# One more convolution tap on TensorE, gate rows folded into weights kept in DRAM, three transposed-input buffers with x loaded a chunk ahead, and softplus at steps 25 and 29

## The reference

```python
mod = (_silu(c) @ wmod).reshape(B, 6, 1, -1)          # sa, ca, ga, sb, cb, gb
ga, gb = (2 * (g >= 0) - 1) * maximum(abs(g), 0.25)   # for both gates
h = _layernorm(x) * (1 + ca) + sa
x = x + ga * mamba(h)
h = _layernorm(x) * (1 + cb) + sb
x = x + gb * (einsum('btd,rde->bte', h, factors) / sqrt(8) + bias)
```

```python
h, gate = split(h @ in_proj.T)
h = silu(causal depthwise conv of 4 taps over time (h) + conv_b)
dt, Bp, Cp = split(h @ x_proj.T)                      # 128, 16, 16
dt = softplus(dt @ dt_proj.T + dt_proj_b)
s  = s * exp(dt * A) + (dt * h) * Bp                  # scan over time, per channel and state
y  = (sum over states of s * Cp + h * D) * silu(gate)
return y @ out_proj.T
```

## Time and profile before

| | |
|---|---|
| median of 3 runs | 2041.11 us (2040.35 to 2041.86) |
| profiled execution | 2039.69 us, its span 2038.0 us |
| VectorE (DVE) busy | 1886.0 us, 93% |
| GpSimd (POOL) busy | 1859.4 us, 91% |
| TensorE (PE) busy | 1753.2 us, 86% |
| ScalarE (ACT) busy | 1501.1 us, 74% |
| granted TensorE clock, mean | 0.956 |
| DMA queue of SyncE | 174.85 MB, 25.2% of 16 engines' span |

### The profile page before, as it was taken

The page is one execution under the profiler, slowest core; times in us unless marked ns, Lnnn a source line. Parts: engine busy times, 40 slices in busy tenths (PEclk is TensorE's granted clock), DMA queues, the critical chain, the costliest instruction groups (busy, mean ns, idle before and its releaser), DMA issues.

```text
span 2038.0 us, 28861 instructions
## 1 busy us (share of the span) xinstructions
PE 1753.2 (86%) x8872; PEld 1288.6 (63%) x8872; DVE 1886.0 (93%) x2343; ACT 1501.1 (74%) x4602; POOL 1859.4 (91%) x924
## 2 busy tenths in 40 slices
PE   7887888989888898988979789798988979799798
PEld 4666656667665666656666575666657666576664
DVE  2898999999999999999999899999999999999995
ACT  3777687776877777787777777777787777877663
POOL 0889999999999999999998999999999999999993
PEclk9898999989999998999999989999999999999798
DMA  4647304041230404123142230404113041310300
GB/s 169 238 84 193 96 31 147 22 155 42 94 99 27 156 22 142 56 79 104 38 145 73 102 109 29 150 27 140 57 72 110 32 145 37 122 60 28 119 27 31
DMA packets 71599, 184.04 MB, mean 90 GB/s; under 512 B 6674, under 2 KB 8338, under 8 KB 63252
## 3 DMA queue, kind: packets, MB, share of 16 engines
q1 hardware_dynamic: 67748, 174.85, 25.2%
q0 software_dynamic: 3696, 7.34, 2.2%
HBM read 172.20 MB, written 9.96 MB: 89 GB/s over the span
## 4 chain that ended last, share of the span: by engine, by line
DVE 32%; ACT 18%; POOL 17%; PE 16%; issue 15%; DMA 1%; DVEq 0%; POOLq 0%; SPq 0%; ACTq 0%
DVE decay L1362 11%; POOL ub L541 9%; DVE state_p L1362 9%; ACT decay L666 6%; POOL state_p L569 5%; DVE sc_d L1377 5%; PE bank_c L1092 4%; PE y_bank L949 3%; ACT dt L772 2%; DVE bank_a L1417 2%; ACT L666 2%; ACT L772 2%; PE bank_a L1039 1%; PE bank_c L1119 1%; ACT xa L681 1%
## 5 line engine op out<-in xcount | busy, mean ns | idle before, releaser
L541 POOL TENSOR_TENSOR ub<-u,b_all 128x2048 f32<-128x2048 f32 x255 | 1164.5, 4567 | 48.2 <-DMA b_all<-bc_scratch 48.2
L666 ACT ACTIVATE decay<-dt,decay_rate 128x256 f32<-128x256 f32 (+1 forms) x2048 | 888.9, 466 | 81.1 <-DVE state_p L1362 78.7
L1362 DVE TENSOR_TENSOR_SCAN decay<-decay,carry,ub 128x512 f32<-128x512 f32 x584 | 725.9, 1274 | 16.9 <-ACT decay L666 15.5
L1362 DVE TENSOR_TENSOR_SCAN state_p<-decay,carry,ub 128x512 f32<-128x512 f32 x440 | 559.5, 1273 | 45.1 <-ACT decay L666 45.1
L569 POOL TENSOR_TENSOR state_p<-state_p,c_all 128x1024 f32<-128x1024 f32 (+2 forms) x256 | 529.2, 2067 | 60.3 <-ACT carry L650 49.6
L949 PE MATMUL y_bank<-ident,sc_d 128*128 128x128 f32 x2336 | 361.4, 289 | 141.9 <-DVE sc_d L1377 141.8
L949 PEld LDWEIGHTS y_bank<-ident,sc_d 128*128 128x128 f32 x2336 | 279.9, 148 | 218.5 <-DVE sc_d L1377 212.4
L1377 DVE TENSOR_TENSOR sc_d<-decay,c_all 128x512 f32<-128x512 f32 x584 | 388.8, 670 | 0.0
L650 ACT ACTIVATE carry<-decay 128x2 f32<-128x2 f32 x584 | 95.7, 164 | 340.0 <-DVE sc_d L1377 340.0
L949 PEld LDWEIGHTS y_bank<-ident,state_p 128*128 128x128 f32 x1760 | 212.4, 146 | 96.1 <-POOL state_p L569 50.6
L949 PE MATMUL y_bank<-ident,state_p 128*128 128x128 f32 x1760 | 248.7, 283 | 26.4 <-POOL state_p L569 23.5
(11 more groups left out here) (138 smaller groups left out, 1858.9 us busy)
## 6 DMA issues: line engine op xcount, KB each, us to landing
win_h<-win_m SPq DMA_DIRECT2D x128, 256.0 KB, 2.6
win_z<-win_m SPq DMA_DIRECT2D x128, 256.0 KB, 2.7
b_all<-bc_scratch SPq DMA_DIRECT2D x31, 1024.0 KB, 6.1
c_all<-bc_scratch SPq DMA_DIRECT2D x31, 1024.0 KB, 7.1
xa<-x SPq DMA_DIRECT2D x16, 512.0 KB, 4.0
xc<-x SPq DMA_DIRECT2D x16, 512.0 KB, 3.7
out<-xc SPq DMA_DIRECT2D x15, 512.0 KB, 6.8
ffn<-factors POOLq DMA_DIRECT2D x7, 1024.0 KB, 9.1
```

What stands on the lines that cost most here:

```text
L541: pool.tensor_tensor(ub[:, slot, :, :, :], u[:, (PAIRS * c + q) % U_PAIRS, :, :].unsqueeze(1).to_broadcast([P, QUAD, 2, ROWS]), b_all[:, n ...
L666: last = act.activation(bk[:, j * ROWS + j:(j + 1) * ROWS], dt[:, pair % DT_PAIRS, j, j:], ACT.Exp, scale=decay_rate[:, e, n:n + 1])
L1362: dve.tensor_tensor_scan(dst, bk[:, :], ub[:, quad % UB_RING, i, :, :].rearrange("p j r -> p (j r)"), carried_in[:, n, 2 * q:2 * q + 1], A ...
```

## The change

- **Taps.** VectorE keeps one tap (`DVE_TAPS = 1`, two instructions a pair), and TensorE has two (`PE_TAPS`, four matmul calls a pair). The diagonals are made on GpSimd before the first chunk (`make_diagonals`), two instructions, and no longer on ScalarE.
- **Split of the C multiplies.** The tuples give GpSimd 27 and 26 units in plain chunks where it had 29 and 28, 19 and 23 in the first two chunks where it had 21 and 26, and 414 in all where it had 440. `EARLY` moves from units 46 and 54 to units 50 and 58.
- **Gates.** ga and gb have no memory of their own: they lie in `y_rows` and `xc` for a while in the first round. In the first two rounds GpSimd multiplies the weights by the second batch entry's gates into spare buffers (`keep_wo`, four, and `keep_ffn`, two), SyncE stores these in DRAM, and GpSimd then scales the weights in place for the first entry (`scale_wo`, `scale_ffn`). In rounds 8 and 9 the finished weights are loaded; nothing is scaled there. The bias is scaled for both entries at once.
- **Inputs.** `hT` has three buffers, and the second layer norm's transposed rows go there and not into `xa`. So x is loaded a chunk earlier: statistics at steps 25, 26 and 28 and `z_before` at step 30 of the round two before its chunk, `turn_x` at step 31, `modulate_before` at step 1, `project_h` at steps 1 to 4 and 7 to 10 (from 5 to 8 and 10 to 13).
- **The pair work of the next chunk** moves three steps up, except in round 0: `copy_h` and `taps` to steps 5, 7, 10, 12, `add_tap` to 6, 8, 11, 13, tanh and `silu_before` to 7, 9, 12, 14. `project_out` stands at steps 9 to 15 (was 8 to 16). `project_dt` starts at step 16, `copy_dt` and `copy_bc` are at 22 and 23 (were 20 and 21), `expand_dt` at 22, 23, 26, 27 (were 19, 20, 23, 24).
- **Softplus** groups are at steps 25 and 29. `stats_before` (two instructions) stands between the two scans of step 25, and `add_ffn(c - 1, 1)` between those of step 29.

```diff
-PE_TAP = 2
-TAP_STEPS = 2 * PE_TAP
+DVE_TAPS = 1
+PE_TAPS = range(DVE_TAPS, TAPS - 1)
+H_RING = 3
+H_LATE = 3
+M_AT = (2, 1)
+IN_AT = ((2, 3, 4, 5, 7, 8, 9, 10), (1, 2, 3, 4, 7, 8, 9, 10))
-EVEN_POOL = (2, 2, 2, 2, 2, 2, 3, 2, 2, 2, 2, 1, 2, 1, 1, 1)
-ODD_POOL = (2, 2, 2, 2, 2, 2, 2, 2, 2, 2, 2, 1, 2, 1, 1, 1)
+EVEN_POOL = (2, 2, 2, 2, 2, 2, 2, 2, 2, 2, 2, 1, 1, 1, 1, 1)
+ODD_POOL = (2, 2, 2, 2, 1, 2, 2, 2, 2, 2, 2, 1, 1, 1, 1, 1)
-EARLY = (46, 54)
+EARLY = (50, 58)
...
+            def keep_wo(i):
+                if i == 0:
+                    pool.wait_ge(wo_loaded, 16)
+                    pool.wait_ge(rows_made, BATCH)
+                wait(pool, wo_stored, 16 * i)
+                pool.tensor_tensor(spare[2], wo[:, 2 * i:2 * i + 2, :], ga[:, 1:2, :].to_broadcast([P, 2, DIM]),
+                                   ALU.mult).then_inc(wo_kept, 1)
...
+            def make_diagonals():
+                pool.wait_ge(prep, 3)
+                pool.wait_ge(consts_made, 1)
+                for i, k in enumerate(PE_TAPS):
+                    pool.tensor_tensor(tap_diag[:, i, :, :], ident[:, :].unsqueeze(1).to_broadcast([P, KE, P]),
+                                       conv[:, :, k:k + 1].to_broadcast([P, KE, P]), ALU.mult).then_inc(diag_made, 1)
...
-                    if c == 0 and g in (7, 9, 11, 13):
-                        scale_wo(0, g // 2 - 3)
-                    if c == PER and g in (11, 12, 13, 14):
-                        scale_wo(1, g - 11)
-                    if c % PER == 1 and g in (4, 5):
-                        scale_ffn(c // PER, g - 4)
+                    if c == 0 and g in (6, 7, 9, 10):
+                        keep_wo({6: 0, 7: 1, 9: 2, 10: 3}[g])
+                    if c == 0 and g in (7, 8, 9, 11):
+                        scale_wo({7: 0, 8: 1, 9: 2, 11: 3}[g])
+                    if c == 1 and g in (2, 4):
+                        keep_ffn(g // 2 - 1)
+                    if c == 1 and g in (3, 5):
+                        scale_ffn(g // 2 - 1)
...
                 for j in range(2):
-                    last = pe.matmul(h_lane(c, q)[:, j * ROWS:(j + 1) * ROWS], tap_diag[:, 2 * q + j, :],
-                                     pre[q % 2][:, j, PE_TAP:PE_TAP + ROWS], start=False, stop=True, skip_group_check=True)
+                    for i, k in enumerate(PE_TAPS):
+                        last = pe.matmul(h_lane(c, q)[:, j * ROWS:(j + 1) * ROWS], tap_diag[:, i, 2 * q + j, :],
+                                         pre[q % 2][:, j, k:k + ROWS], start=False, stop=(k == TAPS - 2),
+                                         skip_group_check=True)
...
+                    if c + 2 < CHUNKS and s == 25:
+                        stats_before(c + 2)
+                    if lc is not None and s == 29:
+                        add_ffn(c - 1, 1)
```

More of the change, by code:

```diff
@@ L429, in one_round @@
                     load_z(c, m)
[L430 to L437, removed]
+                if c >= 2:
+                    load_xc(c - 1)
+                if c + 2 < CHUNKS:
+                    load_xa(c + 2)
                 if c == PER + 1:
@@ new lines, in scale_wo, with keep_ffn @@
+            def scale_wo(i):
+                pool.wait_ge(wo_kept, i + 1)
+                part = wo[:, 2 * i:2 * i + 2, :]
+                pool.tensor_tensor(part, part, ga[:, 0:1, :].to_broadcast([P, 2, DIM]), ALU.mult).then_inc(wo_scaled, 1)
+            def keep_ffn(i):
+                if i == 0:
+                    pool.wait_ge(fac_added, 16 * (RANK - 1))
+                    pool.wait_ge(rows_made, 2 * BATCH)
+                    pool.wait_ge(c_full[1], 2)
+                wait(pool, ffn_stored, 16 * i)
+                pool.tensor_tensor(spare[0], ffn[:, 2 * i:2 * i + 2, :], gb[:, 1:2, :].to_broadcast([P, 2, DIM]),
+                                   ALU.mult).then_inc(ffn_kept, 1)
@@ L600, in one_round @@
                     quad = QUADS * c + g
-                    if la is not None and g == 0:
-                        norm_before(c + 1)
+                    if c == 0 and g == 0:
+                        norm_before(1)
+                    if c + 2 < CHUNKS and g == 13:
+                        norm_before(c + 2)
                     if lc is not None and g == 9:
@@ L773, in soft_dt, with seam_decays @@
                 last.then_inc(dt_made, 1)
-            def seam_decays(c, par):
-                act.wait_ge(dt_made, PAIRS * c + PAIRS)
+            def seam_decays(c, par, half):
+                act.wait_ge(dt_made, PAIRS * c + 2 * half + 2)
                 wait(act, ub_made, QUADS * (c - 1) - 1)
-                for q in range(PAIRS):
+                for q in (2 * half, 2 * half + 1):
                     e, slot = 2 * q + 1, (PAIRS * c + q) % DT_PAIRS
@@ L1240, in one_round @@
                 for s in range(STEPS):
-                    if la is not None and s in (9, 11, 14, 16):
-                        add_tap(c + 1, {9: 0, 11: 1, 14: 2, 16: 3}[s])
+                    a = s - H_LATE if c == 0 else s
+                    if la is not None and a in (6, 8, 11, 13):
+                        add_tap(c + 1, {6: 0, 8: 1, 11: 2, 13: 3}[a])
                     turn_states(STEPS * c + s)
@@ L1410, in taps @@
                 dve.wait_ge(pre_made, PAIRS * c + q + 1)
-                for k in range(PE_TAP):
+                for k in range(DVE_TAPS):
                     for j in range(2):
```

322 lines of the change are left out of this document (174 added, 148 removed).

## The result

The changed kernel takes 2103.3 us (median of 4 runs, 2096.63 to 2109.9) against 2041.11: a ratio of 1.0305, interval 1.0266 to 1.0344. It is 3% slower, where I had forecast 2002 us and a chance of 0.88 for faster. Its profiled execution took 2098.99 us, with a span of 2097.3.

A forecast was written before the change was run, and what follows sets the result against it. VectorE's queue was taken to set the pace, GpSimd hardly behind. Twelve plain rounds -29.3, round 9 -10.4, rounds 0 and 1 +1 sum to -38.7 us: 2002 forecast, own range 1990 to 2012, wider range 1974 to 2028.

The forecast's parts named there:

- costed at nothing: Items given no time: GpSimd's diagonals, lead-in taps, the later B and C round trip, reloads in rounds 8 and 9, tail.
- account of rounds 0 and 1: Gate folding on GpSimd in the first two rounds: 260.5 us together, +1, bounds -4 and +15.
- waits for TensorE in steps 5 to 9: Sign that the forecast is wrong, listed beside no wait at step 12 and others; no size given.
- The rival in which TensorE's order decides: Plain rounds: longer taps before each tanh and the shared steps 1 to 4 give 123.6 us a round, 2070; chance 0.09.
- The waits of a plain round: VectorE's waits in a plain round: 3.7 us against 4.3 before, on 114.7 of work, giving 118.4.
- The third pair: Steps 12 and 13: TensorE's late, longer tap makes VectorE wait 1.4 us for tanh, `pre` or decay; bounds 0 and 3.0.
- The norm in step 19: VectorE's wait for the norm: no term in the plain round's sum, and no such wait expected.
- Step 29: VectorE's wait for ScalarE's decay behind the softplus group, with `add_ffn` in between: 0.6 us, bounds 0 and 1.8.
- the rival in which the waits only move: Plain rounds: the taps' 1.9 us a round return as other VectorE waits, 120.9 a round, 2034 us; chance 0.06.
- The rival with 1977: GpSimd's pace: third pair's lateness hidden, plain rounds at 116.4 us, 1977 in all; chance 0.25.
- the +15 of that rival: Rounds 0 and 1: folding costs its full price, +15 us in place of +1, 2016 in all; chance 0.10.
- Round 9: Loses its `ffn` scaling and the lag from round 8, becoming a plain round: 118.4 us against 128.8, -10.4.

The follow-up runs named there:

- experiment one: Changed kernel with SyncE loading `win_h` tiles 3 to 5 ahead of the gate tiles and both x loads: 2038.71 us, ratio 0.9982 to the kernel before.
- Experiments two to four: Changed kernel, `win_h` tiles 3 to 5 behind the gate tiles: ahead of both x loads, 2040.86 us; behind `xc` only, span 2057.7; behind `xa` only, span 2053.0.
- Experiment six: Kernel of experiment one with the output projection's first four jobs at steps 9, 11, 12, 12, not 9 to 12: 2022.38 us, ratio 0.9911 to the kernel before.
- experiment seven: Kernel of experiment six with one scan product more a round given to GpSimd: span 2019.1 us against 2019.2.
- experiment ten: Changed kernel with all three repairs: late weight tiles first, output projection jobs spread, gate's last tanh ahead of the copy in step 5: 2012.43 us, ratio 0.9863.

## Why the prediction was wrong

**The step that failed** is in the "costed at nothing" and in the account of rounds 0 and 1: I followed SyncE's queue there and in the B and C trip, and nowhere else. The loads of `win_h` in a plain round thus went into the sum at nothing, without a reason. The change moves two things towards each other. The projection of the fourth tile goes from step 8 to step 4, and the load of `xa` goes ahead of the late `win_h` tiles in the queue, where only that of `xc` had been. No sentence of mine asked when the fourth tile lands in a plain round. In its place the runs showed a tile that is 3.6 us late on average in rounds 2 to 14, which costs 58.1 us by experiment one, some 22 of them by the lower clock behind the wait (the estimate above). Experiments two to four show that the bytes in front do it. One of my signs of being wrong was waits for TensorE in steps 5 to 9, and it came, in step 6. The rival in which TensorE's order decides named the moved projection, but for its matmuls and not for its weights. It came nearest to the time, 2070, for another reason, which is luck, and I gave it 0.09.

**The waits of a plain round** are the second step that failed. With the loads put right (experiment one) they are 6.1 us on average over the twelve, and not 3.7. Before the change they were 4.3. Three terms were off:
- The third pair, forecast 1.4, measured 2.3. The mechanism is the one forecast. Seven us of TensorE's work lie between the first of the two projections and the tap (605.22 to 612.54, 7.3 us, the sum that I made), but the first one starts 1.7 us after `silu_before` (603.51) and not 0.7, since the transposes of the states, which end at 605.22, stand in front. That makes the tap a us later than forecast, which is about the missing 0.9. Experiment six removes 1.6 of the 2.3.
- The norm in step 19, forecast 0, measured 1.0. I had only counted the norm of the input side, whose wait did go, and GpSimd's slack of 2.7 us a round. But slack on average doesn't help at one place. GpSimd is behind at step 19. With one product more for it the wait grew from 0.7 to 1.1 us (experiment seven). It may also hang on a carry that it waited for earlier, which I have not shown.
- Step 29, forecast 0.6, measured between 0.46 and 1.56, 0.9 on average.

The waits in step 22 (forecast 0.8, measured 0.89), step 30 (0.3 and 0.2) and step 5 (0.4 and 0.40) came as forecast, step 25 nearly so (0.2 and 0.4). So did the work: a plain round of 120.8 us less its waits of 6.1 is 114.7, as forecast.

With its loads in time, the change is then the rival in which the waits only move: forecast 2034, measured 2038.7, which is still outside my range. VectorE's work falls by the 1.9 us a round that were forecast, its waits rise by 1.9, and the plain rounds are as long as before. The rival with 1977 needed the lateness at the third pair to be hidden, and it was not: 2.3 us of waiting. That GpSimd's work paces the rounds is refuted by experiment seven for the kernel of experiment six.

**Rounds 0 and 1**, forecast 260.5, measured 268.2. Of the +8.8 on before, 3.0 is the late tile in round 1 (127.5 in experiment one). Round 1 is 2.9 us shorter than before without it, and round 0 is 8.7 us longer. I had put GpSimd in round 0 at 126.9 of work and 5 of idle time. It has 126.1 and 11.6, and over 10 of these are waits for a carry, as before the change; I had taken them for waits for the mods and softplus. The idle time that I meant to fill can't be filled by work that stands behind the wait in the same queue. The folding is dear, but at +5.8 it is not the +15 of that rival.

**Round 9** was right in its mechanism, hidden under the late tile: it has become a plain round, 121.8 us beside an average of 120.8 in experiment one and 118.4 beside 118.6 in experiment ten. That its 118.4 is the forecast figure needed the three repairs. **The lead-in** grew by 1.9 where I had 0 for it.

The forecast of 118.4 us for a plain round and -10.4 for round 9 is what the kernel with all three repairs does, and that is partly luck. Its waits sum to 3.9 us a round for the forecast 3.7, but from other terms: 0.7 for 1.4 in step 12, 0.7 for 0 in step 19, 1.1 for 0.6 in step 29 and none for 0.4 in step 5. Of three new latenesses (the tile, the third pair, the norm) I had found one, and priced it too low.

## What to carry to other kernels

When an operation is moved earlier, write down for each of its operands when it now has to be there, and read the queue that brings it: what stands in front, and how many bytes. Here 1 MB in front of a 256 KB tile cost 58 us, more than the 39 that the whole change was forecast to bring. Part of that price was indirect: in 10 of 13 rounds TensorE ran at a lower clock behind its wait. A large transfer that nobody waits for belongs behind a small one that somebody does, and that is an edit of three lines.

When work goes off the engine that seems to be the bound, and the rounds stay as long as they were, list the bound engine's waits by step. In the three places mended here (the late tile, the third pair, the gate's tanh) the cure was the order of another queue, and cost nothing.

## What was not expected of the hardware

The scaling of the bias has two operands in SBUF and 512 elements in a row, on two partitions. VectorE in the changed kernel, round 0:

```profile
144.91 10.14 DVE L1542 SCALAR_TENSOR_TENSOR bias_row<-bias_row,dt 2x512 f32<-2x512 f32 x1
154.98 1.27 DVE L1424 TENSOR_TENSOR_SCAN decay<-decay,carry,ub 128x512 f32<-128x512 f32 x1
```

The kernel before has the same multiply on one partition, and it took 0.67 and 0.89 us. The long one is no accident of one execution: it took 9.94 us in experiment one and 10.07 in experiment eleven.

GpSimd at that time:

```profile
143.72 2.83 POOL L612 TENSOR_TENSOR wo<-wo,y_rows 128x1024 f32<-128x1024 f32 x1
146.04 4.95 POOL L562 TENSOR_TENSOR ub<-u,b_all 128x2048 f32<-128x2048 f32 x1
150.50 1.71 POOL L590 TENSOR_TENSOR state_p<-state_p,c_all 128x512 f32<-128x512 f32 x1
151.72 2.78 POOL L605 TENSOR_TENSOR hT<-wo,y_rows 128x1024 f32<-128x1024 f32 x1
154.58 2.68 POOL L612 TENSOR_TENSOR wo<-wo,y_rows 128x1024 f32<-128x1024 f32 x1
```

**Experiment eleven** put an instruction of this kind, 128 by 128, at steps 11 and 21 of rounds 2 to 15, in the kernel of experiment six:

```
+                    if c >= 2 and s in (11, 21):
+                        dve.scalar_tensor_tensor(out=probe[:, :], in0=tap_diag[:, 0, 0:1, :].rearrange("p k r -> p (k r)"),
+                                                 scalar=2.0, in1=tap_diag[:, 1, 0:1, :].rearrange("p k r -> p (k r)"),
+                                                 op0=ALU.mult, op1=ALU.mult)
```

> The kernel with the output projection's jobs spread, and at steps 11 and 21 of each round from the third on VectorE multiplies two constant tiles of SBUF (128 by 128 each) into an unused one: 28 samples of an instruction of the same kind as the scaling of the bias, which took 10.14 us in the first round for 512 elements in a row. Theory A: such an instruction, with both operands in SBUF, is held up while GpSimd runs instructions back to back: its durations spread from about 0.2 us to several us, and long ones end where a GpSimd instruction ends. Theory B: the 10.14 us belonged to that place (its rows had just been written by a transfer, or GpSimd's instruction there is of another kind) and all samples take 0.2 to 0.4 us; the span then rises by 28 x 0.3, some 8 us.

Measured: span 2029.2, and this row for the tile (ns min, median, max):

```profile
L1633 DVE SCALAR_TENSOR_TENSOR probe<-tap_diag x28: 284/1062/4534, 368.4 to 1958.3; 128x128 f32<-128x128 f32 x28
```

Theory A holds. The 28 samples took 42.9 us together, and the span grew by 10.0. One of the samples, and GpSimd beside it:

```profile
487.13 3.08 DVE L1633 SCALAR_TENSOR_TENSOR probe<-tap_diag 128x128 f32<-128x128 f32 x1
```

```profile
485.52 4.54 POOL L566 TENSOR_TENSOR ub<-u,b_all 128x2048 f32<-128x2048 f32 x1
490.13 0.21 POOL L580 TENSOR_TENSOR ub<-ub,seam 128x4 f32<-128x4 f32 x1
```

It began inside GpSimd's multiply and ended at 490.21, just after that did (490.06). All 28 end 0.14 to 0.22 us after the end of a GpSimd instruction. The short ones, near 0.29 us, are those that began within the last 0.15 us of one. The Trainium skill, "SBUF — State Buffer", section SBUF: two separate sides, has the rule: VectorE with two SBUF inputs and GpSimd reading SBUF take the shared ports for a whole instruction, and the other is blocked. The samples agree with it. By it the bias would have been let in at about 146.5, when the first of GpSimd's instructions ended. It wasn't let in before the fourth had ended, at 154.5. What I can say from the rows is that there the records of GpSimd overlap by some 0.5 us from one to the next (143.72 + 2.83 is 146.55, and the next began at 146.04), while those in progress at the samples and the next ones overlap by 0.06 us at most. The fourth and fifth beside the bias, where VectorE was let in, stand 0.08 us apart. Whether this is what shut VectorE out I have not tried.
